# The last stage of a decoder kernel, an fp8-rounded matrix product with residual and layer norm, rewritten for more engines and two groups of rows in flight

## The reference

```python
x = x.astype(jnp.bfloat16)
x2 = x.reshape(-1, x.shape[-1])                       # 2048 rows of 128
x_q = (x2.astype(jnp.float32) / s_in).astype(jnp.float8_e4m3fn)
k_q = (kernel.astype(jnp.float32) / s_k).astype(jnp.float8_e4m3fn)
y = jnp.dot(x_q.astype(jnp.float32), k_q.astype(jnp.float32)) * (s_in * s_k)
y = y.astype(jnp.bfloat16) + bias
...
x = _layernorm(x + y)                                 # the result of the whole program
```

## Time and profile before

| | us |
|---|---|
| median of 3 runs | 1723.0 (1722.15 to 1731.67) |
| profiled execution, its own time | 1742.72 |
| span of the profiled execution | 1740.8 |
| DVE busy over the span | 1194.6 |
| last instruction of `L3_CROSS` on ACT to the span's end | 1673.4 to 1740.8 |

### The profile page before, as it was taken

How to read it: one execution, slowest core, us unless ns; L and a number is a source line. 1 busy time by engine, 2 the same in 40 slices (tenths; PEclk the granted TensorE clock), 3 DMA queues, 4 the chain that set the end, 5 groups by cost and what they waited for, 6 DMA issues and landing times.

```text
span 1740.8 us, 40909 instructions
## 1 busy us (share of the span) xinstructions
PE 1312.3 (75%) x15370; PEld 909.0 (52%) x15385; DVE 1194.6 (69%) x2584; ACT 698.7 (40%) x1447; POOL 790.3 (45%) x966
## 2 busy tenths in 40 slices
PE   4878859878888877799996886655888761898820
PEld 2656536556656556456664555553555561565510
DVE  4986859963389846389895784134778723898867
ACT  1543435543345533234342452331555520555510
POOL 2553357741177713245552562424556515566610
PEclk9998979997789989799998996786999965999965
DMA  8000000000000000000000001112000013000000
GB/s 317 1 1 1 0 0 1 0 1 20 0 1 0 0 13 0 18 1 0 0 0 1 1 1 30 40 41 108 0 1 1 1 40 32 1 0 1 0 2 24
DMA packets 17871, 30.53 MB, mean 18 GB/s; under 512 B 4213, under 2 KB 14069, under 8 KB 17030
## 3 DMA queue, kind: packets, MB, share of 16 engines
q1 hardware_dynamic: 15878, 25.59, 4.2%
q0 software_dynamic: 1920, 3.94, 1.5%
HBM read 24.54 MB, written 4.98 MB: 17 GB/s over the span
## 4 chain that ended last, share of the span: by engine, by line
PE 42%; DVE 20%; issue 17%; POOL 12%; ACT 5%; DMA 1%; another core or an unknown queue 1%; SPq 1%; POOLq 0%; DVEq 0%; ACTq 0%
PE ps L314 34%; DVE maxima L407 5%; PE ps L430 4%; DVE arena L409 3%; POOL inv_norm L829 3%; PE ps L764 3%; ACT arena L417 2%; POOL arena L494 2%; POOL arena L834 2%; DVE heads_out L706 2%; DVE sq_sum L968 1%; POOL arena L1790 1%; POOL rstd L348 1%; DVE gate L1638 1%
## 5 line engine op out<-in xcount | busy, mean ns | idle before, releaser
L314 PE MATMUL ps<-arena 64*64 64x64 f32 (+5 forms) x7937 | 384.7, 277 | 51.5 <-issue 15.1
L314 PEld LDWEIGHTS ps<-arena 64*64 64x64 f32 (+4 forms) x7937 | 239.3, 132 | 180.4 <-issue 130.4
L494 POOL TENSOR_TENSOR arena<-arena,w_const 128x1024 f32<-128x1024 f32 x96 | 182.5, 1903 | 150.6 <-DVE arena L691 64.8
L407 DVE TENSOR_REDUCE maxima<-ps 128x16 f32<-128x1024 f32 (+1 forms) x144 | 158.6, 1101 | 52.3 <-PE ps L314 49.6
L417 ACT ACTIVATE arena<-arena 128x1024 f32<-128x1024 f32 (+1 forms) x144 | 138.7, 963 | 126.1 <-DVE arena L409 125.4
L430 PE MATMUL ps<-w_const,arena 128*128 128x128 f32 x1024 | 143.2, 281 | 37.5 <-ACT arena L417 32.6
L409 DVE TENSOR_TENSOR arena<-ps,maxima 128x1024 f32<-128x1024 f32 (+1 forms) x144 | 159.3, 1106 | 4.9
L829 POOL TENSOR_TENSOR inv_norm<-sq_floor,minus_half 128x16 f32<-128x16 f32 x32 | 121.9, 3809 | 78.4 <-DVE sq_floor L971 78.4
L424 ACT COPY arena<-ps 128x1024 f32<-128x1024 f32 (+1 forms) x144 | 131.4, 913 | 51.4 <-PE ps L430 50.8
L430 PEld LDWEIGHTS ps<-w_const,arena 128*128 128x128 f32 x1024 | 115.7, 144 | 59.9 <-ACT arena L417 42.7
L348 POOL TENSOR_TENSOR rstd<-var_eps,minus_half 128x1 f32<-128x1 f32 x144 | 79.8, 568 | 140.7 <-DVE var_eps L390 65.6
(11 more groups left out here) (301 smaller groups left out, 2679.8 us busy)
## 6 DMA issues: line engine op xcount, KB each, us to landing
experts<-in_pack_moe SPq DMA_DIRECT2D x2, 4180.0 KB, 19.4
w_fa<-in_pack_fa SPq DMA_DIRECT2D x2, 1024.0 KB, 11.8
moe_in<-state SPq DMA_DIRECT2D x2, 1024.0 KB, 5.4
w_a<-in_pack_a SPq DMA_DIRECT2D x1, 1824.0 KB, 16.9
moe_out<-arena SPq DMA_DIRECT2D x5, 256.0 KB, 2.3
w_fg<-in_pack_fg SPq DMA_DIRECT2D x2, 537.0 KB, 12.3
ctxT<-in_ctxT SPq DMA_DIRECT2D x1, 1024.0 KB, 7.8
out<-state SPq DMA_DIRECT2D x1, 1024.0 KB, 5.1
```

Source lines behind the costliest of these rows:

```text
L314: return nc.tensor.matmul(o, lhsT, rhs, start=start, stop=stop, skip_group_check=True)
L407: nc.vector.reduce_max(mx, sc, X_AXIS).then_inc(signal["max_ready"], 1)
L494: nc.gpsimd.tensor_tensor(keys_wide(s).rearrange("p (b h t) -> p b h t", b=SEQS, h=8), key8(s).rearrange("p (b t) -> p b t", b=SEQS).unsqu ...
```

## The change

Only the last phase is rewritten, with the loads and the store around it.

- Every engine's program of the phase is written out for the 4 groups, with no loop. Most buffers are there twice (`fp_scratch(s)`), for even and odd groups.
- POOL makes the bf16 copy of `state` (L2316 of the new file), adds the bias to the product (L2323) and `state` to that (L2329), does `pow` (L2333), and multiplies it with minus the mean (L2335). It waits for the four tiles of a group, not for the whole phase before.
- ACT scales the input (L2362), makes the square (L2364), doubles the half (L2370), copies the turned group (L2374), scales the product out of PSUM (L2379), and writes the normalized rows (L2386, four times).
- DVE keeps the half, the clamp, the mask, the copy out and the choice, and the statistics. The six instructions for values out of range are replaced by one maximum per row and tile of the squares (128x4) and two instructions of 128x4. What they give is added to the mean and the variance of the row.
- The weights go to a part of `inner` that is free by then, and are loaded right behind the `alibi` table at the end of `F1_GLU`. DVE rounds them with the same number of instructions, before the first group.
- SP stores each group of four tiles when it is finished (four DMAs of 256 KB) and waits for all at the end.

```diff
         def fp8_pool(ph):
-            with pool_engine.Fori(0, GROUPS) as g:
-                group_norm_pool(pool_engine, 2, g)
+            def bf16_input(g):
+                pool.wait_ge(tile_done, 2 + 16 * (ph - 1) + 4 * (g + 1))
+                if g >= 2:
+                    pool.wait_ge(fs["f_in"], 2 * (g - 2) + 2)
+                nc.gpsimd.tensor_copy(fp[g % 2]["x16"], group_of(state, g)).then_inc(fs["f_x16"], 1)
...
         def fp8_scalar(ph):
             act = scalar_engine
-            with act.Fori(0, GROUPS) as g:
+
+            def scaled_input(g):
+                f = fp[g % 2]
+                act.wait_ge(fs["f_x16"], g + 1)
+                if g >= 2:
+                    act.wait_ge(fs["f_max"], 2 * (g - 2) + 1)
+                    act.nop(nofuse=True)
+                nc.scalar.activation(f["x"], f["x16"], ACT.Identity, bias=zero8, scale=inv8[:, 0:1])\
+                    .then_inc(fs["f_in"], 1)
+                nc.scalar.activation(f["size"], f["x16"], ACT.Square, bias=zero8, scale=inv8[:, 0:1])\
+                    .then_inc(fs["f_in"], 1)
...
+            act.wait_ge(fs["f_once"], 3)
+            scaled_input(0)
+            for g in range(GROUPS):
+                large_values(g)
+                if g + 1 < GROUPS:
+                    scaled_input(g + 1)
+                turned_copy(g)
+                if g:
+                    normal(g - 1)
+                scaled_output(g)
+            normal(GROUPS - 1)
...
+            def round_group(g):
+                f = fp[g % 2]
+                dve.wait_ge(fs["f_in"], 2 * g + 1)
+                half, small = split(f["x"], f["half8"], f["small8"])
+                half.then_inc(fs["f_halved"], 1)
+                small.then_inc(fs["f_masked"], 1)
+                dve.wait_ge(fs["f_in"], 2 * g + 2)
+                nc.vector.tensor_scalar(f["mask"], f["size"], SMALL, None, ALU.is_ge)
+                dve.wait_ge(fs["f_masked"], 2 * g + 1)
+                dve.nop(nofuse=True)
+                if g >= 2:
+                    dve.wait_ge(fs["f_turned"], g - 1)
+                nc.vector.tensor_copy(f["q_x"], f["small8"]).then_inc(fs["f_masked"], 1)
+                nc.vector.reduce_max(f["largest"], f["size"].rearrange("p (t d) -> p t d", t=4), X_AXIS)\
+                    .then_inc(fs["f_max"], 1)
+                dve.wait_ge(fs["f_large"], g + 1)
+                dve.wait_ge(fs["f_masked"], 2 * g + 2)
+                nc.vector.copy_predicated(f["q_x"], f["mask"], f["large"]).then_inc(fs["f_rounded"], 1)
...
+            for g in range(GROUPS):
+                round_group(g)
+                if g:
+                    statistics(g - 1)
+            statistics(GROUPS - 1)
...
+            for g in range(GROUPS):
+                sp.wait_ge(tile_done, 2 + 16 * (PHASES - 1) + 4 * (g + 1))
+                sp.dma_start(out.rearrange("(t p) d -> p t d", p=P)[:, 4 * g:4 * g + 4, :], state[:, 4 * g:4 * g + 4, :])\
+                    .then_inc(out_stored, 16)
+            sp.wait_ge(out_stored, 16 * GROUPS)
```

More of the change, by code:

```diff
@@ L2296, in fp8_tensor @@
         def fp8_tensor(ph):
             pe = tensor_engine
-            turned = ps[0][:, 0, :].bitcast(BF16)
-            with pe.Fori(0, GROUPS) as g:
-                pe.wait_ge(fs["f_rounded"], g + 1)
+            for g in range(GROUPS):
+                f, turned = fp[g % 2], ps[g % 2][:, 0, :].bitcast(BF16)
+                pe.wait_ge(fs["f_rounded"], g + 2)
                 for tt in range(4):
-                    last = nc.tensor.transpose(turned[:, tt * P:(tt + 1) * P], q_x[:, tt * P:(tt + 1) * P],
+                    last = nc.tensor.transpose(turned[:, tt * P:(tt + 1) * P], f["q_x"][:, tt * P:(tt + 1) * P],
@@ new lines, in large_values, with turned_copy, scaled_output @@
+            def large_values(g):
+                f = fp[g % 2]
+                act.wait_ge(fs["f_halved"], g + 1)
+                nc.scalar.mul(f["large"], f["half8"], 2.0).then_inc(fs["f_large"], 1)
+            def turned_copy(g):
+                act.wait_ge(fs["f_turned"], g + 1)
+                nc.scalar.copy(fp[g % 2]["q_xT"], ps[g % 2][:, 0, :].bitcast(BF16)[:, 0:GT])\
+                    .then_inc(fs["f_turned_copy"], 1)
+            def scaled_output(g):
+                act.wait_ge(fs["f_y"], g + 1)
+                nc.scalar.activation(fp[g % 2]["y16"], bank(g % 2, 1), ACT.Identity, bias=zero8,
+                                     scale=scale_both).then_inc(fs["f_y16"], 1)
@@ new lines, in normal @@
+            def normal(g):
+                f = fp[g % 2]
+                act.wait_ge(fs["f_bias"], g + 1)
+                for tt in range(4):
+                    nc.scalar.activation(state[:, 4 * g + tt, :], f["acc"][:, tt * D:(tt + 1) * D], ACT.Identity,
+                                         bias=f["bias"][:, tt:tt + 1], scale=f["rstd"][:, tt:tt + 1])\
+                        .then_inc(tile_done, 1)
+            act.wait_ge(fs["f_once"], 3)
[8 more added lines that the diff above has]
+                scaled_output(g)
@@ new lines, in statistics @@
+            def statistics(g):
+                f = fp[g % 2]
+                dve.wait_ge(gs["g_sum"], USES + g + 1)
+                for tt in range(4):
+                    last = nc.vector.bn_stats(f["stats"][:, 6 * tt:6 * tt + 6], f["acc"][:, tt * D:(tt + 1) * D])
+                last.then_inc(gs["g_stats"], 1)
+                dve.wait_ge(gs["g_stats"], USES + g + 1)
+                if g >= 2:
+                    dve.wait_ge(fs["f_bias"], g - 1)
+                dve.nop(nofuse=True)
+                for tt in range(4):
+                    last = nc.vector.bn_aggr(f["moments"][:, 2 * tt:2 * tt + 2], f["stats"][:, 6 * tt:6 * tt + 6])
+                last.then_inc(gs["g_mean"], 1)
+                dve.wait_ge(gs["g_mean"], USES + g + 1)
+                mean, var = (f["moments"].rearrange("p (t m) -> p t m", m=2)[:, :, k:k + 1].rearrange("p t m -> p (t m)")
+                             for k in range(2))
+                nc.vector.scalar_tensor_tensor(out=f["minus_mean"], in0=mean, scalar=-1.0, in1=f["nan"],
+                                               op0=ALU.mult, op1=ALU.add)
+                nc.vector.scalar_tensor_tensor(out=f["var"], in0=var, scalar=EPS, in1=f["nan"],
+                                               op0=ALU.add, op1=ALU.add).then_inc(gs["g_var"], 1)
```

161 lines of the change are left out of this document (81 added, 80 removed).

## The result

The changed kernel takes 1703.9 us as the median of 4 runs, and the kernel before, measured with it, 1727.3. The ratio is 0.9859, with a 95% interval of 0.9831 to 0.9887, so 23.5 us or 1.4% less. The prediction was 1700 us in a range of 1690 to 1708, 23 us less than before.

What follows compares the result with a forecast made beforehand. The DVE queue was taken as the bound, with an unhidden DMA at either end. First output 1680.6, three rings of 8.26, collision 2.1, 7.55 more and the last store give a 1717.7 span, 23.1 us under 1740.8: 1700 us, range 1690 to 1708.

Steps and rivals of the forecast that it cites:

- What is at stake: Last phase only: 68.1 us, 4% of the span, can change; nothing before 1672.7 us should move.
- one of the prediction's own signs: Phases ahead of the last: the prediction is wrong if phases before 1672.7 us change their times.
- The early weights: Start of last phase: loads cost nothing, DVE's 5.68 us wait goes, its 15 weight instructions take 3.67 us, to 1674.9.
- The first output: Group 0 from POOL's cast to ACT's scaling out of PSUM: first output y0 there at 1680.6 us.
- The ring: Each group: output waits for previous output, two additions, statistics, `pow` and product, four norms; 8.26 us in all.
- The other way round: Ring via additions, cast of group g+2, scaling and square, turned copy, norm: shorter, 2.8 against 3.0 us behind the additions.
- The collision: DVE's choice against POOL's additions on shared SBUF ports: each waits for the other, three times, 2.1 us in all.
- The end: After y3: 7.55 us to 1715.0, then a 256 KB store landing in 2.3 us; span ends at 1717.7.
- two groups are truly in flight: Rival for the last phase: ring doesn't bind, ACT does at 5.3 us a group; 11 us less, 1689; chance 0.03.
- The rivals with dearer or cheaper prices: Last phase: dearer POOL additions, casts and collision, 1708, chance 0.15; cheaper additions, ACT and no collision, 1690, chance 0.17.
- a late arrival of straight code: Rival: the last phase's straight code arrives some 4 us a group late, gain lost, 1716 us; chance 0.03.
- a slow POOL on bf16: Rival: POOL's 8 additions with bf16 operands are slow; at 6 us each the kernel takes 1738 us; chance 0.02.

Runs made afterwards that it cites:

- e1: Changed kernel with ACT issuing the output of group g ahead of the four norms of group g-1: last phase 38.8 us, against 44.75 in the changed kernel.
- e2: Changed kernel with ACT's doubled half of group g+1 issued right behind the turned copy of group g: last phase 42.85 us, against 44.75.
- e3: Changed kernel with the three weight loads back at their old place, behind the end of the phase before: last phase 49.9 us, against 44.75.
- e8: Changed kernel with the doubled half early on ACT and both additions (bias, state) on DVE instead of POOL: last phase 38.2 us, against 44.75.
- e9: Changed kernel with doubled half early, output ahead of norms on ACT, and POOL's `pow` and product mostly one turn later: last phase 42.1 us, against 44.75.
- e4: Changed kernel with one 1 MB store at the end in place of four by groups: last phase 46.8 us, against 44.75.
- e6: Kernel before without its five DVE instructions for values out of range (L2334 to L2338), nothing in their place: last phase 54.2 us, against 68.1.
- e10: Changed kernel with doubled half early and output ahead of norms on ACT, both additions on DVE: last phase 31.9 us, median 1685.35 against 1698.6.

## Why the prediction was right

By its own steps, measured in the changed kernel's profile:

- **What is at stake.** Only the last phase moved in a way that belongs to the change, 68.1 to 44.75. The forecast was 45.0 (1717.7 - 1672.7). By one of the prediction's own signs it would be wrong, since the phases ahead of 1672.7 did change their times, by 16.4 us between the two profiles. That is the standstill, 18.5 us, less 2.1 us elsewhere, and e1, e2, e3, e8 and e9 show that the changed kernel can have it too. The absolute time was 4 us over 1700 because the median of the kernel before, with a fourth run, is 4 us above the 1723.0 that the forecast was taken from.
- **The early weights.** No cost, and the wait gone, as said. DVE's 15 instructions took 4.1 us rather than 3.67 (1654.73 to 1658.87), because some stood still beside POOL's casts: L2467 took 0.64, and 0.22 in e3, where the casts were over. They did come last before the first rounding. e3 prices the edit at 5.2 us.
- **The first output.** Casts 0.6 (0.63 said), scaling and square 0.81 and 0.80 (0.81), output 0.78 (0.76). It was finished 8.0 us behind the last bias; 7.9 was said.
- **The ring.** It is there, closed by the order on ACT, and e1 shows that this order binds. The other way round was shorter, as said: it takes over in e1, at 7.0 us. The additions were dearer in the forecast (1.28 each) than they are (1.15 undisturbed). Four norms took 1.65 (1.67), the statistics 1.6 (1.73), `pow` and product 1.02 and 0.20 (1.29).
- **The collision.** It happened where it was said to, but its size came out another way. The choice makes the second addition 0.33 us longer, not 0.69: it ends only 0.47 us behind the start of that addition, so the addition does not wait out its whole length. DVE's small flag instructions wait for the addition and the cast and put the statistics back by 0.5 us, and `pow` is 0.28 longer beside the rounding of the next group. That makes 1.1 us a group in place of 0.7, where a cast follows, and 0.4 where none does. Cheaper additions and a dearer collision cancelled, which was luck: 8.91 and 8.90 us against 8.96 with it. The third step had 8.29. I had overlooked that DVE's instructions on 4 columns are held up by POOL as much as those on 512.
- **The end.** The way out of the last group took 7.2 us (7.55). The store went the other way: 3.49 us from the last norm to the end of the span, where I said 2.7. The landing was 2.3 us as said, but about 0.8 us more passed at the end of the program than before (SP's queue waited 1.0 us for PE's there, 0.2 in the kernel before). e4 prices the edit at 2.0, not 2.8.

The terms that were off were about 1 us or less each, over the whole phase, and of both signs. The two edits that were run by themselves, weights and store, are worth 5.2 and 2.0 us of the 23.3; 16.1 remain for less work on DVE and for the spreading over engines. Of these, e6 gives the first some 9.3 us by subtraction. What the spreading is worth by itself no run shows.

The rival that two groups are truly in flight was rightly given little. But its price, 11 us less, was the useful part. Opening the ring on ACT alone gave 6.0 us (e1), because another one stands close behind it. e10, with two moves in ACT's order and the additions on DVE, gets 12.9 us more out of the same buffers, and there DVE binds and not ACT. The rivals with dearer or cheaper prices came only in part (additions 1.15 instead of 1.28, a dearer collision); a late arrival of straight code or a slow POOL on bf16 did not come at all. The chances of the cases that the prediction counts as faster add up to 0.95 by themselves, not to 0.94 with a part of a fifth.

## What to carry to other kernels

Two sets of buffers don't put two groups in flight; the order of each queue does. Follow one output backwards through the queues, and if the path comes round to the output before it, the loop's length is the time of a group, whatever the engines' busy shares. When work is moved from VectorE to GpSimd, look at what it now stands beside: here the two additions cost 2.3 to 2.6 us on GpSimd and 1.1 on VectorE, and moving them back was a gain once VectorE had time to spare.

## What the runs showed of the hardware

- A DVE instruction on 128x4, which takes 0.17 us alone, took 1.11 beside a POOL addition of 128x512 and ended with it. That an instruction is short doesn't protect it. The Trainium skill (SBUF — State Buffer, Who interferes with whom) puts `tensor_scalar` among the operations that can take the shared ports when their operands meet certain conditions. The 1.11 us fit that, but no row shows whether these operands meet the conditions.
- DVE's rounding of the next group made POOL's `pow` on 4 columns 1.30 instead of 1.02 us, a loss of 0.28. That is what DVE's first rounding instruction (L2411, from 1678.03 for 0.42 us) still had to run when `pow` started at 1678.19; the later ones ran beside `pow` at their usual 0.42. In `L1_ATTN` the loser had stood for a whole microsecond.
- GpSimd added bf16 operands (L2323) at the same 1.15 us as float ones with a bf16 operand (L2329), and cast 128x512 float to bf16 in 0.60 us.
- The first expert phase takes 46 us or 61 to 65 us to its first store, by series of runs. The difference of 15 to 19 us is most of what this change is worth, so a single profile on either side can't price it.
